# Loading the constants first and running the first chunk's step size, input product and first scan tile by tile

## The chip, the cores and the metric

The kernel runs on one core of a Trainium2 chip. What counts is the device time of one execution in microseconds; the time given for a kernel is the median of its runs.

## What is computed

x holds 2 sequences of 1024 tokens of 256 features. Rows of small norm are masked, a Mamba block (in-projection, causal convolution, selective scan with 16 states, gate, out-projection) runs on them, then an attention block with a modulated query and a gated feed-forward. The part that the change touches is the front of the Mamba block:

```python
rows_to_keep = clip((sigmoid(cond @ score_w + score_b) * 1024).astype(int32), 1, None)
thresholds = sort(norm(x))[::-1][rows_to_keep - 1]          # rows below are zeroed
xn = rmsnorm(x_masked, rms_w)
xi, z = split(xn @ in_proj, 2)                              # 512 channels each
xi = silu(causal_conv4(xi) + conv_b)
dt, Bm, Cm = split(xi @ x_proj, [16, 32])
delta = softplus(dt @ dt_w + dt_b)
A = -exp(A_log)
def step(h, (d_t, x_t, B_t, C_t)):                          # over time, h: 512 x 16
    h = exp(d_t[..., None] * A) * h + (d_t * x_t)[..., None] * B_t[:, None, :]
    return h, einsum('bds,bs->bd', h, C_t)
y = (scan(step) + xi * D) * silu(z)
```

## The kernel before

Time is cut into four chunks of 512 steps (NCH = 4, two per sequence), the 512 channels into four tiles of 128 (CT = 4), and a chunk's scan into 16 states (NS). One scan step n is one state of one chunk: for each of the four tiles ScalarE makes exp(delta * A) into one of two PSUM banks (L1259), GpSimd makes the input product dx * B into a ring of four slots (L1403), and VectorE runs the scan over 512 steps of time (L1727). TensorE turns the result (L834), ScalarE and VectorE multiply it by C's column (L1269, L1740 and L1747), and TensorE or VectorE sums over the states.

TensorE's other work is a list of jobs, each with a PSUM bank. Jobs alternate between two banks of `pp`, so a job waits until the one two places ahead of it has been read. The head's list is: T (transposes of x), F (the keep fraction), I (in-projection), V (convolution), X (x_proj), D 0 to D 3 (the step size before softplus), XT (B and C turned; its reading by ScalarE writes `CTs`, the rows of C). Z 0 and Z 1 (the gate's in-projection) stand beside step 0, Z 2 and Z 3 beside step 1. So XT waits for the reading of D 2, Z 0 for that of D 3, Z 1 for that of XT, and Z 2 for that of Z 0.

Every engine works its instructions off in the order in which they are written. In the head: SP loads x's first two chunks (L421), the vectors (L425), the constants with the identity matrix (L426), and then weights; TensorE first runs WARM_ZEROS products on zeros (L863), the transposes T, and the transposes of the squared norms (L857), which need four sums of squares from ScalarE and four from VectorE. VectorE counts with them which rows are kept (L1652). `first_softplus` on ScalarE takes D 0 and D 1 as a pair, then D 2 and D 3 (Abs at L1117 or L1120, Exp L1122, Ln L1124). VectorE's reading of D (L1538) ends softplus, and behind each pair one instruction multiplies by xi (L1543) for GpSimd. B's rows go over DRAM: SP writes them (L440) and loads them spread over the partitions, two states at a time (L448). Behind the four scans of step 0 VectorE reads Z 0 and Z 1 (L1530), then makes the mask row (L1703) and one count (L1652), and then scans step 1.

## Time and profile before

| | |
|---|---|
| median of 3 runs | 565.59 us (562.24 to 568.28) |
| the profiled execution's own time | 562.97 us |
| its span | 561.2 us |
| mean granted TensorE clock in the span | 0.929 |
| busy: TensorE matmuls, VectorE, GpSimd, ScalarE | 86%, 82%, 69%, 66% |
| chain that ended last: TensorE, VectorE, issue, ScalarE, GpSimd | 49%, 27%, 11%, 10%, 2% |

The share of busy time is that of an engine in the whole span. The chain is followed back from the last instruction to what released each step; an engine with a large share there sets the time. A granted clock of 1 is 2.4 GHz and one of 0.5 is 1.2 GHz.

### The profile page before, as it was taken

The page shows a single profiled execution, that of the slowest core. Times are in us where ns is not written, and L with a number is a line of the kernel's source. Part 1 is how long each engine was busy: PE and PEld are TensorE (multiplying, and loading weights), DVE is VectorE, ACT ScalarE, POOL GpSimd, SP SyncE. Part 2 cuts the span into 40 slices and gives each one's busy share as a digit, 9 for nine tenths or more (in the row PEclk, how much of TensorE's full clock was granted, in tenths as well). Part 3 has the DMA queues.
Part 4 walks back from the last instruction along what each step waited for, and adds up shares of the span by engine and source line. Part 5 has one row for each costly group of instructions (what it writes and reads, how often), then busy time and mean ns, then how long its engine had stood idle before and what let it go on. Part 6 is the DMA issues. An engine that isn't in the chain of part 4 may idle for free.

```text
span 561.2 us, 7944 instructions
## 1 busy us (share of the span) xinstructions
PE 481.0 (86%) x2777; PEld 348.8 (62%) x2777; DVE 461.2 (82%) x531; ACT 372.5 (66%) x650; POOL 387.2 (69%) x235
## 2 busy tenths in 40 slices
PE   8968999868768999987689999986897968899992
PEld 6423765455557665745576657656796856888651
DVE  4779989979999889799997897899998989851522
ACT  3676777769966767898757678897568668721210
POOL 5039978767996877879968778599789969510001
PEclk9987999979989999899899999598998869799997
DMA  8330111111111001111010111111111590029004
GB/s 289 115 116 38 39 38 39 40 40 37 39 37 39 38 39 39 40 39 39 39 39 37 39 37 41 38 38 38 39 39 39 201 369 1 2 87 353 2 1 155
DMA packets 17919, 38.88 MB, mean 69 GB/s; under 512 B 1665, under 2 KB 10497, under 8 KB 17874
## 3 DMA queue, kind: packets, MB, share of 16 engines
q1 hardware_dynamic: 17874, 38.32, 19.8%
q8 instruction: 24, 0.39, 0.3%
q14 instruction: 21, 0.17, 0.1%
HBM read 36.08 MB, written 2.23 MB: 68 GB/s over the span
## 4 chain that ended last, share of the span: by engine, by line
PE 49%; DVE 27%; issue 11%; ACT 10%; POOL 2%; DVEq 0%; ACTq 0%; POOLq 0%
DVE scanmem L1727 16%; PE hT L834 11%; PE pp L563 6%; PE pp L539 6%; PE yacc L597 5%; DVE yTd L1747 5%; PE pp L626 4%; ACT dA L1259 2%; PE dA L799 2%; PE pp L575 2%; PE pp L589 2%; ACT hc L1269 1%; PE pp L770 1%; PE pp L649 1%; DVE yTd L1652 1%
## 5 line engine op out<-in xcount | busy, mean ns | idle before, releaser
L1403 POOL TENSOR_TENSOR scanmem<-par,scanmem 128x1024 f32<-128x1024 f32 x128 | 300.9, 2370 | 79.7 <-PE hT L834 60.3
L834 PE MATMUL hT<-con,scanmem 128*128 128x128 f32 x1024 | 167.4, 298 | 54.0 <-DVE yTd L1747 32.0
L1259 ACT ACTIVATE dA<-par,Aneg 128x512 f32<-128x512 f32 x256 | 171.7, 690 | 56.0 <-DVE scanmem L1727 54.5
L834 PEld LDWEIGHTS hT<-con,scanmem 128*128 128x128 f32 x1024 | 126.7, 152 | 108.2 <-issue 34.3
L1727 DVE TENSOR_TENSOR_SCAN scanmem<-dA,carry,scanmem 128x512 f32<-128x512 f32 x128 | 156.7, 1266 | 11.9 <-ACT dA L1259 11.7
L1727 DVE TENSOR_TENSOR_SCAN scanmem<-dA,scanmem 128x512 f32<-128x512 f32 x128 | 148.9, 1204 | 8.5 <-ACT dA L1259 7.8
L1269 ACT ACTIVATE hc<-hT,CTs 128x512 f32<-128x512 f32 x128 | 87.1, 680 | 43.5 <-PE hT L834 43.3
L597 PE MATMUL yacc<-con,hc 128*128 128x128 f32 x512 | 86.6, 297 | 0.3 <-ACT hc L1269 0.3
L597 PEld LDWEIGHTS yacc<-con,hc 128*128 128x128 f32 x512 | 69.4, 157 | 0.6 <-ACT hc L1269 0.6
L1747 DVE SCALAR_TENSOR_TENSOR yTd<-hT,CTs,yTd 128x512 f32<-128x512 f32 x85 | 62.0, 729 | 8.4 <-PE hT L834 7.5
L539 PE MATMUL pp<-xnT,wi 128*128 128x512 f32 x120 | 59.0, 620 | 3.4 <-ACT xnT L1038 2.1
L563 PE MATMUL pp<-xr,diag 128*128 128x512 f32 x112 | 50.2, 592 | 0.0
L1463 POOL TENSOR_TENSOR par<-xt,hc 128x1024 f32<-128x1024 f32 x1 | 2.4, 2350 | 53.0 <-ACT hc L1319 53.0
L539 PEld LDWEIGHTS pp<-xnT,wi 128*128 128x128 f32 x120 | 21.6, 198 | 22.2 <-issue 17.4
L563 PEld LDWEIGHTS pp<-xr,diag 128*128 128x128 f32 x112 | 20.3, 189 | 21.1 <-issue 20.9
L626 PE MATMUL pp<-wo,par 128*128 128x256 f32 x128 | 29.0, 381 | 0.5 <-DVE par L1507 0.5
L1415 POOL TENSOR_TENSOR yTd<-yTd,sm 128x512 f32<-128x512 f32 x21 | 26.9, 1280 | 0.0
L626 PEld LDWEIGHTS pp<-wo,par 128*128 128x128 f32 x128 | 23.8, 190 | 3.9 <-DVE par L1507 0.7
L1415 POOL TENSOR_TENSOR yTd<-yTd,xnT 128x512 f32<-128x512 f32 x14 | 17.8, 1274 | 8.1 <-ACT xnT L1278 8.1
L589 PE MATMUL pp<-dbc,wdt 17*128 17x512 f32 x28 | 17.3, 706 | 0.4 <-DVE xt L1553 0.3
L1538 DVE SCALAR_TENSOR_TENSOR par<-pp,par 128x512 f32<-128x512 f32 x14 | 9.6, 688 | 9.3 <-ACT par L1130 6.4
L799 PE MATMUL dA<-con 128*128 128x128 f32 x110 | 17.1, 289 | 0.0
(195 smaller groups left out, 510.8 us busy)
## 6 DMA issues: line engine op xcount, KB each, us to landing
scanmem<-brow SPq DMA_DIRECT2D x32, 512.0 KB, 3.6
par<-in SPq DMA_DIRECT2D x1, 4096.0 KB, 17.3
scanmem<-in SPq DMA_DIRECT2D x1, 4096.0 KB, 15.0
xt<-in SPq DMA_DIRECT2D x4, 512.0 KB, 6.7
wi<-in SPq DMA_DIRECT2D x2, 1024.0 KB, 6.7
out<-par SPq DMA_DIRECT2D x4, 512.0 KB, 4.1
aw<-in SPq DMA_DIRECT2D x5, 256.0 KB, 6.7
xr<-in SPq DMA_DIRECT2D x1, 1024.0 KB, 8.9
```

The costliest lines, as they stand in the source:

```text
L539: last = mm(o, win[:, k, col:col + P], xnT[:, k, :], start=k == 0, stop=k == KD - 1)
L563: last = mm(o, dg[:, m, k, :], xr3[:, m, k:k + T], start=k == 0, stop=k == KC - 1)
L589: return mm(o, wdt[:, m * P:(m + 1) * P], dbc[0:DR + 1, :], start=True, stop=True)
L597: return mm(o[:, m * P:(m + 1) * P], src, ident, start=False, stop=last, is_transpose=True, skip_group_check=True)
L626: last = mm(o[:, i * DM:(i + 1) * DM], dx(e)[:, m, t0:t0 + P], wo[:, m, :], start=m == 0, stop=m == CT - 1)
L834: last = nc.tensor.transpose(hT[:, i % 2, m * P:(m + 1) * P], hb[:, n % RING, m, i * P:(i + 1) * P], ident)
L1259: A(dA[:, m % 2, :], delta(c)[:, m, :], ACT.Exp, scale=Aneg[:, m * NS + s:m * NS + s + 1]).then_inc(da_ready, 1)
L1269: A(hc[:, e % 2, :], hT[:, 0, :], ACT.Copy, scale=CTs[:, c % 2, i, s:s + 1]).then_inc(mul_done, 1)
L1403: nc.gpsimd.tensor_tensor(hb[:, n % RING, ms, :], dx(c)[:, ms, :], Bb[:, row:row + 1, :].to_broadcast([P, 2, T]), ALU.mult).then_inc(bx_re ...
L1415: nc.gpsimd.tensor_tensor(dst, dst, for_pool(n), ALU.add).then_inc(pool_sum_done, 1)
L1727: V.tensor_tensor_scan(hb[:, n % RING, m, :], dA[:, m % 2, :], hb[:, n % RING, m, :], start, ALU.mult, ALU.add).then_inc(scan_done, 1)
L1747: V.scalar_tensor_tensor(dst, src, cs, dst, ALU.mult, ALU.add).then_inc(mac_done, 1)
```

## The change

Five things are changed.

- SP loads the constants first of all, ahead of x, on a semaphore of their own (`s_con`). TensorE's transposes wait for that one alone; ScalarE waits for the vectors ahead of its reading of T, GpSimd for the vectors and then for the constants.
- WARM_ZEROS is 5 instead of 8.
- `first_softplus` takes one tile at a time; VectorE multiplies each tile by xi by itself, and GpSimd makes the first input product of step 0 in four instructions of one tile (`first_input_step`) instead of two of two tiles.
- The exponentials and scans of step 0 are moved in between those tiles.
- ScalarE reads XT (C's rows) behind the four exponentials of step 0 instead of ahead of them.

```diff
-WARM_ZEROS = 8
+WARM_ZEROS = 5
...
+            sp.dma_start(con[:, :], consts).then_inc(s_con, 16)
             load_x(0)
             load_x(1)
             sp.dma_start(vec[:, :], vecs).then_inc(s_vec, 16)
-            sp.dma_start(con[:, :], consts).then_inc(s_vec, 16)
...
-            def first_softplus(pair):
+            def first_softplus(m):
 
-                d = delta(0)[:, 2 * pair:2 * pair + 2, :]
-                if pair == 0:
-                    for m in range(2):
-                        wait_full(act, ("D", 0, m))
-                        own.mark(A(delta(0)[:, m, :], bank(("D", 0, m)), ACT.Abs))
-                else:
-                    wait_full(act, ("D", 0, 3))
-                    own.mark(A(d, hT[:, :, :], ACT.Abs))
+                d = delta(0)[:, m, :]
+                wait_full(act, ("D", 0, m))
+                own.mark(A(d, bank(("D", 0, m)), ACT.Abs))
...
+            first_softplus(0)
+            first_softplus(1)
+            exp_step(0, 0)
+            first_softplus(2)
+            exp_step(0, 1)
+            first_softplus(3)
+            exp_step(0, 2)
+            exp_step(0, 3)
+            read(("XT", 0, 0))
...
+            def first_input_step():
+
+                pool.wait_ge(bb_in[0], 16)
+                for m in range(CT):
+                    pool.wait_ge(dx_ready, m + 1)
+                    nc.gpsimd.tensor_tensor(hb[:, 0, m, :], dx(0)[:, m, :], Bb[:, 0, :], ALU.mult).then_inc(bx_ready, 1)
...
-                if n == 0 and m % 2:
-                    wait_read(dve, ("D", 0, m - 1))
+                if n == 0:
                     wait_read(dve, job)
-                    ms = slice(m - 1, m + 1)
-                    V.tensor_tensor(dx(0)[:, ms, :], delta(0)[:, ms, :], xi(0)[:, ms, :], ALU.mult).then_inc(dx_ready, 2)
+                    V.tensor_tensor(dx(0)[:, m, :], delta(0)[:, m, :], xi(0)[:, m, :], ALU.mult).then_inc(dx_ready, 1)
...
+            read(("D", 0, 0))
+            read(("D", 0, 1))
+            scan_step(0, 0)
+            read(("D", 0, 2))
+            scan_step(0, 1)
+            read(("D", 0, 3))
+            scan_step(0, 2)
+            scan_step(0, 3)
```

ScalarE around the first softplus, before, from the Abs of D 0 and D 1 to the reading of Z 0 and Z 1 (L1117 to L1124 softplus, L1089 C's rows, L1259 the exponentials of step 0, L1102 the tanh of Z with its table load):

```order
L1117 ACTIVATE par<-pp 128x512 x2
L1122 ACTIVATE par<-par 128x1024
L1124 ACTIVATE par<-par 128x1024
L1120 ACTIVATE par<-hT 128x1024
L1122 ACTIVATE par<-par 128x1024
L1124 ACTIVATE par<-par 128x1024
L1089 ACTIVATE CTs<-pp 128x64
L1259 ACTIVATE dA<-par,Aneg 128x512 x4
L1102 ACT_TABLE_LOAD
L1102 ACTIVATE par<-pp 128x512 x2
```

The same place in the changed kernel, behind the softplus of D 0 and D 1 (L1120 to L1124 softplus, L1255 the exponentials, L1094 C's rows, L1107 Z):

```order
L1255 ACTIVATE dA<-par,Aneg 128x512
L1120 ACTIVATE par<-hT 128x512
L1122 ACTIVATE par<-par 128x512
L1124 ACTIVATE par<-par 128x512
L1255 ACTIVATE dA<-par,Aneg 128x512
L1120 ACTIVATE par<-hT 128x512
L1122 ACTIVATE par<-par 128x512
L1124 ACTIVATE par<-par 128x512
L1255 ACTIVATE dA<-par,Aneg 128x512 x2
L1094 ACTIVATE CTs<-pp 128x64
L1107 ACT_TABLE_LOAD
L1107 ACTIVATE par<-pp 128x512 x2
```

Two exponentials now stand ahead of the end of softplus, and C's rows are read behind all four.

VectorE before, from the reading of D 0 to the mask row (L1538 the reading of D, L1543 the product with xi, L1727 the scans of step 0, L1530 the reading of Z, L1703 the mask row, L1652 a count):

```order
L1538 SCALAR_TENSOR_TENSOR par<-pp,par 128x512 x2
L1543 TENSOR_TENSOR par<-par 128x1024
L1538 SCALAR_TENSOR_TENSOR par<-hT,par 128x512 x2
L1543 TENSOR_TENSOR par<-par 128x1024
L1727 SCALAR_TENSOR_TENSOR scanmem<-dA,scanmem 128x512 x4
L1530 SCALAR_TENSOR_TENSOR par<-par,pp 128x512 x2
L1703 TENSOR_SCALAR negm<-x1T 128x1024
L1652 TENSOR_SCALAR yTd,cnt<-x1T,ss 128x1024
```

VectorE in the changed kernel, from the reading of D 1 on (L1556, L1559, L1742, L1548 and L1716 are the same things in the same order):

```order
L1556 SCALAR_TENSOR_TENSOR par<-pp,par 128x512
L1559 TENSOR_TENSOR par<-par 128x512
L1742 SCALAR_TENSOR_TENSOR scanmem<-dA,scanmem 128x512
L1556 SCALAR_TENSOR_TENSOR par<-hT,par 128x512
L1559 TENSOR_TENSOR par<-par 128x512
L1742 SCALAR_TENSOR_TENSOR scanmem<-dA,scanmem 128x512
L1556 SCALAR_TENSOR_TENSOR par<-hT,par 128x512
L1559 TENSOR_TENSOR par<-par 128x512
L1742 SCALAR_TENSOR_TENSOR scanmem<-dA,scanmem 128x512 x2
L1548 SCALAR_TENSOR_TENSOR par<-par,pp 128x512 x2
L1716 TENSOR_SCALAR negm<-x1T 128x1024
```

The reading of D 3 now stands behind the first two scans.

## Rows read from the trace of the kernel before

**Rows 1.** The page: its first line, the span.
```profile
span 561.2 us, 7944 instructions
```

**Rows 2.** The chain that ended last, in order of time: start us, us, what.
```profile
9.71 1.30 DVE yTd L1652 x2
...
16.13 0.65 PE hT L876 x4
...
55.52 0.73 DVE yTd L1740
```

**Rows 3.** Timeline of ScalarE: start us, us, instruction; the last sum of squares.
```profile
7.28 0.18 ACT L1203 ACTIVATION_READ_ACCUMULATOR scanmem<-xt 128x1 f32 x1
```

**Rows 4.** Timeline of TensorE: products on zeros; first weight loads of L857.
```profile
1.51 6.41 PE L863 MATMUL hT<-a_sb 128*128 128x256 f32 x16 [1.51 <-POOL z_sb L1369]
...
8.52 0.90 PEld L857 LDWEIGHTS yacc<-con,ss 128*128 128x128 f32 x8
```

**Rows 5.** Timeline of SP's queue: issue of x, of the constants, of B's rows.
```profile
0.74 1.01 SPq L421 DMA_DIRECT2D xt<-in  x2
...
2.33 0.43 SPq L426 DMA_DIRECT2D con<-in  x1
...
34.92 1.28 SPq L448 DMA_DIRECT2D scanmem<-brow  x3
```

**Rows 6.** Timeline of ScalarE, from the first Abs to the reading of Z.
```profile
34.58 0.60 ACT L1117 ACTIVATE par<-pp 128x512 f32<-128x512 f32 x1 [0.31 <-PE pp L589]
...
40.24 1.06 ACT L1124 ACTIVATE par<-par 128x1024 f32<-128x1024 f32 x1
...
47.60 1.28 ACT L1102 ACT_TABLE_LOAD   x1
48.89 1.08 ACT L1102 ACTIVATE par<-pp 128x512 f32<-128x512 f32 x2
```

**Rows 7.** Groups by line and shape, ScalarE: busy us, mean ns | idle before.
```profile
L1130 ACT ACTIVATE par<-par 128x512 f32<-128x512 f32 x12 | 7.6, 630 | 0.4
```

**Rows 8.** Timeline of VectorE, from the first product with xi to the mask row.
```profile
39.74 1.23 DVE L1543 TENSOR_TENSOR par<-par 128x1024 f32<-128x1024 f32 x1
41.40 1.29 DVE L1538 SCALAR_TENSOR_TENSOR par<-hT,par 128x512 f32<-128x512 f32 x2 [0.44 <-ACT par L1124]
42.83 1.73 DVE L1543 TENSOR_TENSOR par<-par 128x1024 f32<-128x1024 f32 x1
...
47.08 2.34 DVE L1727 TENSOR_TENSOR_SCAN scanmem<-dA,scanmem 128x512 f32<-128x512 f32 x2 [0.28 <-POOL scanmem L1403]
49.59 1.28 DVE L1530 SCALAR_TENSOR_TENSOR par<-par,pp 128x512 f32<-128x512 f32 x2 [0.18 <-ACT par L1102]
50.80 1.35 DVE L1703 TENSOR_SCALAR negm<-x1T 128x1024 f32<-128x1024 uint8 x1
```

**Rows 9.** DMA issues by line: KB each, median us from issue to landing.
```profile
scanmem<-brow SPq DMA_DIRECT2D x32, 512.0 KB, 3.6
```

**Rows 10.** Groups by line and shape, GpSimd: a product of one tile.
```profile
L1440 POOL TENSOR_TENSOR par<-par 128x512 f32<-128x512 f32 x12 | 15.1, 1284 | 0.0
```

**Rows 11.** Timeline of TensorE: Z 0 and Z 1, then Z 2 and Z 3.
```profile
42.75 6.27 PE L539 MATMUL pp<-xnT,wi 128*128 128x512 f32 x8
50.34 3.70 PE L539 MATMUL pp<-xnT,wi 128*128 128x512 f32 x8 [1.32 <-DVE par L1530]
```

**Rows 12.** Stretches: each engine's busy us (instructions), then granted clock, DMA share, GB/s.
```profile
47.50:48.00 0.50, 0.50 (x2) 0.02 (x2) 0.50 (x1) 0.48 (x2) 0.50 (x1) 0.55 0.00 0
```

**Rows 13.** Timeline of TensorE from 116 us, and the granted clock of two stretches there.
```profile
116.76 1.11 PE L834 MATMUL hT<-con,scanmem 128*128 128x128 f32 x4 [3.75 <-DVE yTd L1747]
117.67 1.06 PE L597 MATMUL yacc<-con,hc 128*128 128x128 f32 x4
...
116.00:117.00 1.00, 0.24 (x1) 0.24 (x2) 1.00 (x3) 0.90 (x2) 0.02 (x1) 0.61 0.00 0
...
119.00:120.00 1.00, 1.00 (x7) 0.86 (x5) 0.78 (x1) 1.00 (x3) 0.28 (x1) 0.69 0.04 16
```

More of the change, by code:

```diff
@@ L168, in vector_sums, with products_of_inputs @@
     return 2 * n + (i + 1) // 2 - pool_sums(n if i == 3 else n - 1)
+def products_of_inputs(n, pair):
+    return CT + 2 * (n - 1) + pair + 1
 def to_read(h):
@@ L329, in build @@
         brow = nc.dram_tensor("brow", [NCH, NS, T], F32, kind="Internal").ap()
-        s_vec, s_w, s_aw, s_mrow = sem("vec_in"), sem("w_in"), sem("aw_in"), sem("mrow_in")
+        s_vec, s_con, s_w, s_aw, s_mrow = sem("vec_in"), sem("con_in"), sem("w_in"), sem("aw_in"), sem("mrow_in")
         s_x = [sem(f"x_in{i}") for i in range(NCH)]
@@ L444, in _ @@
                     if piece >= BSLOTS:
-                        sp.wait_ge(bx_ready, 2 * BROWS * (piece - BSLOTS + 1))
+                        sp.wait_ge(bx_ready, products_of_inputs(BROWS * (piece - BSLOTS + 1) - 1, 1))
                     slot = piece % BSLOTS
@@ L495, in job_F @@
             def job_F(job, o):
-                pe.wait_ge(s_vec, 32)
+                pe.wait_ge(s_vec, 16)
                 for b in range(B):
@@ L526, in job_T @@
                         pe.wait_ge(s_x[0], 16)
-                        pe.wait_ge(s_vec, 32)
+                        pe.wait_ge(s_con, 16)
                     for i in range(NT):
@@ L1210, in _ @@
             A(xr3[:, :, 0:KC - 1], zero[:, :, :], ACT.Copy).then_inc(halo_ready, 1)
+            act.wait_ge(s_vec, 16)
             for k in range(KD):
@@ L1225, in _ @@
             A(fr[:, 1, :], fr[:, 0, :], ACT.Exp, scale=-1.0).then_inc(fe_ready, 1)
-            act.wait_ge(s_vec, 32)
             A(Aneg[:, :], v("A_log"), ACT.Exp).then_inc(aexp_ready, 1)
@@ L1243, in _ @@
                 A(magrow[:, i * 512:(i + 1) * 512], hT[:, i, :], ACT.Copy).then_inc(mag_act, 1)
-            for pair in range(CT // 2):
-                first_softplus(pair)
-            read(("XT", 0, 0))
             def exp_step(n, m):
@@ L1288, in _ @@
                     n = c * NS + s
-                    exp_step(n, 0)
-                    exp_step(n, 1)
+                    if n:
+                        exp_step(n, 0)
+                        exp_step(n, 1)
                     if n >= 2:
@@ L1296, in _ @@
                         read(job)
-                    exp_step(n, 2)
-                    exp_step(n, 3)
                     if n:
+                        exp_step(n, 2)
+                        exp_step(n, 3)
                         mul_step(n - 1, 0)
@@ L1369, in _ @@
             nc.gpsimd.memset(z_sb[:, :, :], 0.0).then_inc(pads_zero, 1)
-            pool.wait_ge(s_vec, 32)
+            pool.wait_ge(s_vec, 16)
             nc.gpsimd.tensor_scalar(half_b[:, :], v("conv_b"), 0.5, 1.0, ALU.mult, ALU.mult).then_inc(half_ready, 1)
             nc.gpsimd.tensor_scalar(half_w[:, :], v("conv_w"), 0.5, 1.0, ALU.mult, ALU.mult).then_inc(half_ready, 1)
+            pool.wait_ge(s_con, 16)
             for m in range(CT):
@@ L1446, in _ @@
                         row_scaling(c + 1)
-                    input_step(n, 0)
+                    if n:
+                        input_step(n, 0)
                     if n >= RING:
                         add_step(n - RING)
-                    input_step(n, 1)
+                    if n:
+                        input_step(n, 1)
+                    else:
+                        first_input_step()
                     for m in POOL_ENDS:
@@ L1536, in ev_D @@
                 else:
-                    dve.wait_ge(head_sp_ready, m // 2 + 1)
+                    dve.wait_ge(head_sp_ready, m + 1)
                 V.scalar_tensor_tensor(delta(n)[:, m, :], o, 0.0, delta(n)[:, m, :], ALU.max, ALU.add).then_inc(freed(job), 1)
-                if n == 0 and m % 2:
-                    wait_read(dve, ("D", 0, m - 1))
+                if n == 0:
                     wait_read(dve, job)
-                    ms = slice(m - 1, m + 1)
-                    V.tensor_tensor(dx(0)[:, ms, :], delta(0)[:, ms, :], xi(0)[:, ms, :], ALU.mult).then_inc(dx_ready, 2)
+                    V.tensor_tensor(dx(0)[:, m, :], delta(0)[:, m, :], xi(0)[:, m, :], ALU.mult).then_inc(dx_ready, 1)
                 return None
@@ L1695, in _ @@
             V.tensor_scalar(Aneg[:, :], Aneg[:, :], -1.0, None, ALU.mult).then_inc(A_ready, 1)
-            for m in range(CT):
-                read(("D", 0, m))
             def batch1_rows(s):
@@ L1717, in scan_step @@
                 dve.wait_ge(da_ready, i + 1)
-                if m % 2 == 0:
-                    dve.wait_ge(bx_ready, 2 * n + m // 2 + 1)
+                if n == 0:
+                    dve.wait_ge(bx_ready, m + 1)
+                elif m % 2 == 0:
+                    dve.wait_ge(bx_ready, products_of_inputs(n, m // 2))
                 if c % HALVES:
@@ L1751, in _ @@
                     n = c * NS + s
-                    scan_step(n, 0)
-                    scan_step(n, 1)
+                    if n:
+                        scan_step(n, 0)
+                        scan_step(n, 1)
                     if n:
@@ L1757, in _ @@
                         read(job)
-                    scan_step(n, 2)
-                    scan_step(n, 3)
                     if n:
+                        scan_step(n, 2)
+                        scan_step(n, 3)
                         mac_step(n - 1, 3)
```

## The prediction

> **What bounds the kernel now.** I read the page first, then the chain of waits from its start to 60 us, then the timelines of the single engines around each piece of that chain that the change touches, and last the granted clock. The page gives a span of 561.2 us [rows 1]. The change touches only the first 50 us, so the question is how much earlier (or later) the steady loop starts.
>
> The chain in the head starts with the warm-up products on zeros and the eight transposes of x. Behind them come the transposes of the squared norms, L857, and the counting on VectorE, L1652, from 9.71 [rows 2]. What could have been first? ScalarE's last sum of squares reads out at 7.28 plus 0.18, so 7.46 [rows 3]; the squares alone would have let L857 begin there. It began at 8.52 (its first weight load [rows 4]), because the eight products on zeros and the transposes were still in TensorE's queue. From the counting on, everything up to the step-size products follows in one chain.
>
> The end of the head is a second place. VectorE runs without a pause from the Z readings L1530 at 49.59, over the mask row L1703 at 50.80, to the first sum L1740 at 55.52, which the chain names and behind which TensorE goes on with its transposes [rows 2, 8]. The scans of state 0 are ahead of all this. So the loop is released by the time at which VectorE has read Z 0 and Z 1, and not by the scans alone.
>
> **The change part by part: the loads and the zeros.** Three of eight products on zeros go. Each is two instructions, and the sixteen took 6.41 us [rows 4], 0.40 each for 256 columns, nearly what 512 columns take at full clock further on (0.46, eight in 3.70 [rows 11]); so the clock was low for most of them, though the view of the granted clock has no entry that early. Three are worth 2.4 us of TensorE's queue. x is then what is waited for: the transposes end before the squares do. L857 can start at 7.46 plus the delay that the constants now give x. On SP the two loads of x took 1.01 us to issue and the one of the constants 0.43 [rows 5]; a load put ahead delays the others by about 0.45. Gain: 8.52 - 7.46 - 0.45 = 0.6 us. Bounds: 1.06 if x is not delayed at all, 0.16 if it is delayed by twice that. The waits that are moved (ScalarE on the vectors before it reads the transposes; GpSimd on vectors, then constants) come due at about the time x does; 14 us of later work cover GpSimd's diagonals. The early I products need not be quicker: their results wait for the counting.
>
> **The first softplus, tile by tile.** Before, a pair takes an Abs of 0.60 for each tile and an Exp and a Ln of 1.06 for both [rows 6]. Now each tile takes Abs 0.60, Exp 0.63 and Ln 0.63 (the 512-wide form of later chunks, of which the Ln is shown; the Exp has the same mean [rows 7]), 1.9 us with the handovers. In the old run's times:
> - tile 0: Abs at 34.58, Ln done at 36.50; VectorE reads it (0.69) and multiplies (0.62, half of 1.23) until 37.9 [rows 8].
> - tile 1: Ln done 38.3. First exponential for the scan (0.69) until 38.95. Rows of B: the load of them was issued at 34.92 [rows 5] and lands 3.6 us later [rows 9], 38.5, so GpSimd can start its first tile there, 1.28 us each [rows 10], and ends at about 39.7.
> - VectorE: tile 1 until 39.9 (its product slows when GpSimd runs: the second one took 1.73 against 1.23 [rows 8]), first scan 40.0 to 41.2, tile 2 until 42.7, second scan to 43.95.
> - tile 3: Ln done at 43.24 (behind tile 2 and the second exponential), but VectorE reads it only behind the second scan: 43.95 to 44.64. Then its product to 45.3, third scan to 46.6, fourth (behind GpSimd's tile 3, 46.8) to 48.05.
>
> What VectorE and GpSimd take from each other is a disputed price. The row shows 0.5 us more for 1024 columns while GpSimd worked beside it [rows 8], so 0.25 for a tile, and I count it once; two such products stand ahead of the reading of tile 3. Bounds: nothing, or a whole GpSimd instruction of 1.28 for each of the two [rows 10], which makes tile 3 2.3 us later than my walk. The Trainium skill, GPSIMD Engine Reference, 8. Key points, says that GpSimd shares its SBUF interfaces with VectorE and contends with its instructions that have two SBUF inputs, and gives no size; if the two took turns entirely, the sum would be at the upper bound, by the row it is near the lower. The rule speaks against a change that puts such products of both engines side by side, and the trace agrees that there is a price.
>
> The four scans ended at 49.42 before (the last two started at 47.08 and took 2.34 [rows 8]). They are 1.4 us earlier, 2.0 with the gain above. That is what the change buys on VectorE.
>
> **What it costs.** Z 0 uses the PSUM bank that tile 3 of D leaves. Before, VectorE left tile 3 at 42.69 [rows 8] and Z 0 and Z 1 started at 42.75. Now tile 3 is left at 44.64, behind two scans: 1.95 us later. C's rows are read behind the fourth exponential, at 44.7, just in time for Z 1. TensorE had done little for five microseconds, its clock was at half and came back only at 47.9, so the two jobs took 6.27 us, where Z 2 and Z 3, the same eight products, took 3.70 at full clock [rows 11, 12]. With the same 6.27 they end at 50.97. ScalarE's reading (0.60) and VectorE's (0.67, and handovers) follow: 52.3, where before VectorE was through at 50.87, because ScalarE, with its table load from 47.60 to 48.88 behind the last exponential, was nearly as late as Z [rows 6]. The scans' gain is idle time of VectorE now: it waits for Z 1. Sum: +1.45 - 0.6 = **+0.85 us**. Bounds of the disputed term: with 3.70 for the two jobs Z 1 is ready at 48.4, and the sum is -1.7; the first products still run at half clock after such an idle time in this trace, and I take the row of these very jobs.
>
> 562.97 + 0.85 = 563.8 on the scale of the profiled execution. It lies 2.6 us under the median of the three runs, 565.59 (562.24 to 568.28), so the forecast is 566.4. A difference within 1% (5.7 us) is about what a measurement of this kernel can't tell from none, and the largest gain that I can construct in the head is 1.06 + 1.4 = 2.5 us.
>
> **The rivals.**
> 1. The forecast: Z 1 is late, the scans' gain is lost, no measurable difference. 566.4. Chance 0.42.
> 2. The clock comes back early in Z 0, or stays up: VectorE has Z 1 read at about 49.1 instead of 50.87: -1.7 us, 561.2 for the profile, 563.9. For it: when the clock rises has no fixed relation to these jobs. Against: in the trace the jobs had run for 5.2 us when it rose [rows 12]. Chance 0.25.
> 3. Slower, the clock in the head: fewer zeros leave TensorE quiet between the transposes and L857, and the clock is low from there. L857 takes twice 0.89, and the first I pair as long as the Z pair, 6.27 instead of 3.70 [rows 11]. It decides if that pair ends later than 15.5, when TensorE can turn the rows' scale (16.13 before [rows 2], less the gain): from about 10.5 it would end at 16.8, 1.3 late. With 0.9 for L857 the head loses 2.2 against my sum: +3, or 568.6. Against: at 116.76 TensorE began, at half clock behind a long pause, a stretch of turning only (L834, L597), and at 119.6 the clock rose to full [rows 13]; the same kind of work, the transposes, now stands behind the five products on zeros. Chance 0.12.
> 4. Slower, VectorE against GpSimd: both products ahead of the reading of tile 3 wait for a whole GpSimd instruction, 2.3 us; Z 0 and Z 1 follow by as much: +3.1, 568.7. It decides once the products of VectorE take more than about 1.2 instead of 0.62. Against: the row's 0.5 for 1024 columns. Chance 0.06.
> 5. The head does not change: the constants ahead delay x by a whole microsecond, so that the zeros gone gain nothing, and Z is late: +1.45, 567.0. Chance 0.07.
> 6. A shift of the loop moves TensorE's stretches at half clock. The table's mean clock of 0.929 is 14% of the span, 80 us, at half; a tenth or so of that more or fewer, with some of TensorE's work in it on the chain, is a few microseconds; the three runs of before already spread over 6 us. This alone can carry the time past 1%, to either side. Chance 0.08.
>
> **How the numbers follow.** Cases 1, 2 and 5 lie between 563.9 and 567, cases 3 and 4 near 568.6; the spread of single runs is 3 us to each side. The range for 8 in 10 is 561.5 to 570. Over 1% faster (below 559.9) only case 6 with luck, or case 2 together with a fast median: 0.05. Over 1% slower (above 571.2): case 6, or case 3 or 4 with a slow median: 0.06. Within 1%: 0.89.
>
> **What would show it.** L857's first weight load near 7.9; counting on VectorE from about 9.1 (step one). The first scan about 4 us earlier than 44.47, and four scans with gaps between them (step two). Z 0 starting at about 44 behind the reading of tile 3 of D, and VectorE idle before its reading of Z 1, with TensorE named as the releaser (step three). The mask row at about 51.6 against 50.80: if it comes at 49 or earlier, the step on the clock was wrong; if L1652 starts later than 9.7, the step on the loads or zeros was.

## The result, and the profile after

Twenty runs of each kernel on one chip: 562.44 us before (558.79 to 568.57), 566.48 us after (563.0 to 571.83), ratio 1.0091 with an interval of 1.0066 to 1.0116. The ratio and the table of the experiments leave out those runs of a kernel that lie over 1.5% above its fastest (here 5 of before and 2 of after), and so the ratio gives 5.1 us (3.7 to 6.5) where the medians of all twenty lie 4.0 apart. The change thus stays under the 1% that I had set as the limit of a difference, but it is slower: the whole interval lies above 1. The forecast of 566.4 was met by luck: the three runs of before that I started from had a median 3 us above that of twenty. I had forecast +0.85 us, and the change costs five to six times that.

The profiled execution of after is its slowest of twenty (571.83), so its end is not compared with before's. I compare places in the first chunk, above all the end of the fourth scan of a step: from step 4 to step 9 its distance to the same place in before's profile stays the same within 0.01 us in every profile, so it tells how far the head has moved the steps behind it. For after it is +4.05 us.

The chain that ended last, of the changed kernel (start us, us, what):

```profile
8.07 1.09 PE yacc L862 x8
...
11.50 5.37 PE dA L544 x8
16.86 0.44 PE hT L881 x4
...
44.04 1.22 DVE scanmem L1742
45.25 0.59 DVE par L1556
45.89 9.20 PE pp L544 x16
...
56.57 2.25 DVE scanmem L1742 x2
58.82 0.65 DVE yTd L1755
```

The Z jobs (L544, four of them without a pause) stand in the chain, behind VectorE's second scan and its reading of D 3 (L1556). In the chain before, the two first scans of step 0, an exponential of ScalarE, its table load and its reading of Z 0 stood in that place, and only Z 2 and Z 3 behind them. The other end of the piece, the first sum (L1755), starts at 58.74 in the timeline where it was 55.52 [rows 2].

The timeline of VectorE there (start us, us, instruction, idle time before it and what ended it):

```profile
41.59 1.22 DVE L1742 TENSOR_TENSOR_SCAN scanmem<-dA,scanmem 128x512 f32<-128x512 f32 x1 [1.23 <-POOL scanmem L1417]
...
44.04 1.22 DVE L1742 TENSOR_TENSOR_SCAN scanmem<-dA,scanmem 128x512 f32<-128x512 f32 x1
45.17 0.67 DVE L1556 SCALAR_TENSOR_TENSOR par<-hT,par 128x512 f32<-128x512 f32 x1
45.87 0.69 DVE L1559 TENSOR_TENSOR par<-par 128x512 f32<-128x512 f32 x1
46.48 1.22 DVE L1742 TENSOR_TENSOR_SCAN scanmem<-dA,scanmem 128x512 f32<-128x512 f32 x1
48.00 1.22 DVE L1742 TENSOR_TENSOR_SCAN scanmem<-dA,scanmem 128x512 f32<-128x512 f32 x1 [0.31 <-POOL scanmem L1417]
50.40 0.69 DVE L1548 SCALAR_TENSOR_TENSOR par<-par,pp 128x512 f32<-128x512 f32 x1 [1.18 <-ACT par L1107]
52.34 0.69 DVE L1548 SCALAR_TENSOR_TENSOR par<-par,pp 128x512 f32<-128x512 f32 x1 [1.25 <-ACT par L1107]
52.95 2.42 DVE L1716 TENSOR_SCALAR negm<-x1T 128x1024 f32<-128x1024 uint8 x1
55.29 1.27 DVE L1668 TENSOR_SCALAR_CACHE_REDUCE yTd<-x1T,ss 128x1024 f32<-128x1024 f32 x1
...
56.49 2.33 DVE L1742 TENSOR_TENSOR_SCAN scanmem<-dA,scanmem 128x512 f32<-128x512 f32 x2
58.74 0.72 DVE L1755 TENSOR_SCALAR yTd<-hT,CTs 128x512 f32<-128x512 f32 x1
```

These rows answer to [rows 8]. The scans end at 49.22, hardly before the old 49.42. Then VectorE idles 1.18 and 1.25 us ahead of its two readings of Z (before 0.18), and the mask row (L1716) starts at 52.95 against 50.80 and takes 2.42 us against 1.35.

ScalarE, which VectorE waits for, itself waits for TensorE (against [rows 6]):

```profile
46.72 1.28 ACT L1107 ACT_TABLE_LOAD   x1
49.70 0.60 ACT L1107 ACTIVATE par<-pp 128x512 f32<-128x512 f32 x1 [1.70 <-PE pp L544]
51.65 0.60 ACT L1107 ACTIVATE par<-pp 128x512 f32<-128x512 f32 x1 [1.34 <-PE pp L544]
```

TensorE (against [rows 4, 11]): the weight loads of L862, the first I pair, the Z jobs, and the two halves of step 0's transposes:

```profile
8.07 0.85 PEld L862 LDWEIGHTS yacc<-con,ss 128*128 128x128 f32 x8 [1.49 <-ACT scanmem L1203]
...
11.50 5.37 PE L544 MATMUL dA<-xnT,wi 128*128 128x512 f32 x8 [1.00 <-issue]
...
45.89 9.18 PE L544 MATMUL pp<-xnT,wi 128*128 128x512 f32 x16 [1.78 <-DVE par L1556]
54.91 1.04 PE L839 MATMUL hT<-con,scanmem 128*128 128x128 f32 x8
59.51 1.80 PE L839 MATMUL hT<-con,scanmem 128*128 128x128 f32 x8 [3.57 <-DVE yTd L1755]
```

Stretches (each engine's busy us and instructions, then the granted clock, DMA share, GB/s):

```profile
15.00:16.00 1.00, 1.00 (x3) 0.48 (x2) 0.46 (x3) 0.00 (x0) 0.00 (x0) 0.57 1.10 348
...
48.00:50.00 2.00, 2.00 (x3) 0.77 (x3) 1.22 (x1) 0.30 (x2) 2.00 (x1) 0.50 0.00 0
50.00:52.00 2.00, 2.00 (x6) 0.88 (x5) 0.69 (x1) 0.66 (x2) 2.00 (x2) 1.00 0.00 0
...
62.50:63.00 0.50, 0.50 (x4) 0.50 (x4) 0.50 (x2) 0.08 (x2) 0.50 (x1) 0.50 0.00 0
```

The Z jobs run at half clock until about 50. The transposes behind VectorE's first sum start after a pause of 3.57 us (before: 1.38), and for some 3 us from 60 on the clock is at half, which it was not before: the eight transposes take 1.80 against 1.35.

SP's loads of B's rows (against [rows 5]):

```profile
35.44 1.28 SPq L453 DMA_DIRECT2D scanmem<-brow  x3
```

GpSimd's products (L1417 a tile of step 0, L1410 a pair of later steps), each piece as it stands in the timeline of a window:

```profile
39.78 1.70 POOL L1417 TENSOR_TENSOR scanmem<-par,scanmem 128x512 f32<-128x512 f32 x1 [6.14 <-DMA scanmem<-brow]
...
50.16 4.66 POOL L1410 TENSOR_TENSOR scanmem<-par,scanmem 128x1024 f32<-128x1024 f32 x2
...
52.47 5.11 POOL L1410 TENSOR_TENSOR scanmem<-par,scanmem 128x1024 f32<-128x1024 f32 x2
```

The two pair products of the first of these rows start at 50.16 and end at 54.82 (the second starts at 52.47); the last row holds that second one and the next, and the next alone thus takes 5.11 - 2.31 = 2.80 us, where the others take 2.35. That next one is the one that runs when the mask row ends, at 52.95 + 2.42 = 55.37. Why this matters is the second half of this document.

### The profile page after: what moved, and what is told of

The parts are those of the page before. It is cut to its first block, busy times and chain, and to the rows that moved or that the text cites. A ratio compares the mean times of both kernels' runs of the same rounds, so it can differ in the third digit from the quotient of the medians.

```text
span 570.0 us, 7942 instructions
## 1 busy us (share of the span) xinstructions
PE 491.1 (86%) x2771; PEld 356.2 (62%) x2771; DVE 463.0 (81%) x533; ACT 373.7 (66%) x655; POOL 387.9 (68%) x237
## 4 chain that ended last, share of the span: by engine, by line
PE 54%; DVE 22%; issue 10%; ACT 8%; POOL 4%; DMA 1%; DVEq 0%; SPq 0%; ACTq 0%; POOLq 0%
PE hT L839 13%; DVE scanmem L1742 13%; PE pp L544 7%; PE pp L568 6%; PE yacc L602 6%; DVE yTd L1762 4%; PE pp L631 4%; PE pp L594 3%; POOL scanmem L1410 2%; ACT dA L1255 2%; PE dA L804 2%; PE pp L580 2%; PE pp L775 1%; PE pp L654 1%; PE yacc L598 1%
## 5 line engine op out<-in xcount | busy, mean ns | idle before, releaser
L1410 POOL TENSOR_TENSOR scanmem<-par,scanmem 128x1024 f32<-128x1024 f32 x126 | 296.1, 2368 | 78.7 <-PE hT L839 69.0
L839 PE MATMUL hT<-con,scanmem 128*128 128x128 f32 x1024 | 170.0, 302 | 52.4 <-DVE yTd L1762 29.6
L1255 ACT ACTIVATE dA<-par,Aneg 128x512 f32<-128x512 f32 x256 | 171.8, 690 | 57.0 <-DVE scanmem L1742 53.9
L839 PEld LDWEIGHTS hT<-con,scanmem 128*128 128x128 f32 x1024 | 130.1, 155 | 107.4 <-issue 39.2
L1742 DVE TENSOR_TENSOR_SCAN scanmem<-dA,carry,scanmem 128x512 f32<-128x512 f32 x128 | 156.9, 1269 | 11.6 <-ACT dA L1255 11.3
L1742 DVE TENSOR_TENSOR_SCAN scanmem<-dA,scanmem 128x512 f32<-128x512 f32 x128 | 149.4, 1209 | 10.1 <-ACT dA L1255 8.2
L602 PE MATMUL yacc<-con,hc 128*128 128x128 f32 x512 | 88.5, 302 | 0.3 <-ACT hc L1265 0.3
L602 PEld LDWEIGHTS yacc<-con,hc 128*128 128x128 f32 x512 | 70.6, 159 | 0.6 <-ACT hc L1265 0.6
L544 PE MATMUL pp<-xnT,wi 128*128 128x512 f32 x120 | 58.9, 620 | 3.9 <-ACT xnT L1043 2.1
L544 PEld LDWEIGHTS pp<-xnT,wi 128*128 128x128 f32 x120 | 22.0, 203 | 22.3 <-issue 16.8
L594 PE MATMUL pp<-dbc,wdt 17*128 17x512 f32 x28 | 21.0, 845 | 0.4 <-DVE xt L1569 0.3
L1556 DVE SCALAR_TENSOR_TENSOR par<-pp,par 128x512 f32<-128x512 f32 x14 | 9.7, 691 | 9.5 <-ACT par L1130 7.9
```

The costliest lines, as they stand in the source:

```text
L544: last = mm(o, win[:, k, col:col + P], xnT[:, k, :], start=k == 0, stop=k == KD - 1)
L594: return mm(o, wdt[:, m * P:(m + 1) * P], dbc[0:DR + 1, :], start=True, stop=True)
L602: return mm(o[:, m * P:(m + 1) * P], src, ident, start=False, stop=last, is_transpose=True, skip_group_check=True)
L839: last = nc.tensor.transpose(hT[:, i % 2, m * P:(m + 1) * P], hb[:, n % RING, m, i * P:(i + 1) * P], ident)
L1255: A(dA[:, m % 2, :], delta(c)[:, m, :], ACT.Exp, scale=Aneg[:, m * NS + s:m * NS + s + 1]).then_inc(da_ready, 1)
L1410: nc.gpsimd.tensor_tensor(hb[:, n % RING, ms, :], dx(c)[:, ms, :], Bb[:, row:row + 1, :].to_broadcast([P, 2, T]), ALU.mult).then_inc(bx_re ...
```

## The experiments

"B's load" is where SP issues the first load of B's rows (before 34.92), "scans" where the two first scans of step 1 start (before 53.27), "step 9" the distance to before at the end of its fourth scan. Below the first row the ratio is of 12 runs of the kernel (6 of tiles_only) against 29 or 35 of before beside them.

| kernel | ratio to before, interval | B's load | mask row: start, us | scans | step 9 |
|---|---|---|---|---|---|
| after | 1.0091 [1.0066, 1.0116] | 35.44 | 52.95, 2.42 | 56.49 | +4.05 |
| after_zeros8 | 1.0062 [1.0021, 1.0103] | 35.04 | 51.59, 2.85 | 55.55 | +2.80 |
| head_only | 1.0007 [0.9963, 1.0051] | 34.84 | 50.72, 1.34 | 53.18 | -0.08 |
| tiles_only | 1.0101 [1.0038, 1.0164] | 34.30 | 52.44, 1.79 | 55.35 | +2.09 |
| d3_first | 1.0020 [0.9978, 1.0062] | 35.61 | 52.12, 2.55 | 55.78 | +3.35 |
| mask_first | 0.9997 [0.9963, 1.0030] | 34.87 | 48.57, 1.61 | 52.50 | +0.72 |
| early_rows | 0.9987 [0.9953, 1.0021] | 34.37 | 34.95, 0.69 | 52.21 | -0.69 |
| before_early_rows | 0.9968 [0.9935, 1.0001] | 34.26 | 34.83, 0.69 | 50.13 | -1.63 |
| after_warm | 1.0085 [1.0056, 1.0114] | 34.78 | 51.98, 2.74 | 55.84 | +3.29 |
| before_swap | 1.0071 [1.0032, 1.0111] | 34.78 | 51.86, 2.47 | 54.25 | +1.61 |
| after_swap | 1.0052 [1.0012, 1.0093] | 34.69 | 52.78, 1.30 | 54.00 | +0.73 |
| combined | 0.9994 [0.9953, 1.0035] | 34.85 | 35.42, 0.68 | 50.54 | -1.39 |

The head by itself does not come out the same from execution to execution. Of the edits below only the zeros and the order of the loads act ahead of B's load, and yet it is issued at 34.26 to 35.04 in the six profiles with eight zeros. So up to 0.8 us of a distance at step 9 need not be the edit's. Less the difference at B's load it is 3.53 for after, 2.68 for after_zeros8, 2.71 for tiles_only, 2.66 for d3_first, 1.75 for before_swap and 0.96 for after_swap.

**The two halves of the change.** after_zeros8 puts the zeros back:

```diff
-WARM_ZEROS = 5
+WARM_ZEROS = 8
```

> The changed kernel with WARM_ZEROS back at 8, all else as changed. Theory Z (the slowdown comes from the readings: tile 3 of D is read behind two scans, so Z 0, Z 1 and the mask row come late): little changes, still 0.6 to 1.0% over the kernel before; the mask row starts 2 us later than before's 50.80 less what the head gains. Theory H (the slowdown comes from too few products on zeros: the clock falls at about 12 us and the first I pair takes 5.4 us instead of 3.7): the I pair takes 3.7 in the profile and the time comes back to within 0.4% of before.

head_only is the kernel before with the constants loaded first and five zeros:

```diff
-WARM_ZEROS = 8
+WARM_ZEROS = 5
...
+            sp.dma_start(con[:, :], consts).then_inc(s_con, 16)
             load_x(0)
             load_x(1)
             sp.dma_start(vec[:, :], vecs).then_inc(s_vec, 16)
-            sp.dma_start(con[:, :], consts).then_inc(s_vec, 16)
...
```

> The kernel before with the head part alone: constants first and WARM_ZEROS 5, softplus in pairs as before. Theory Z: no slower than before, 0 to 0.2% faster, because the counting starts 0.5 us earlier. Theory H: slower by 0.3 to 0.9%, with the first I pair at 5.4 us and the turning of the rows' scale at 16.7 instead of 16.1.

tiles_only is the rest of the change, with the loads and the eight zeros as before:

```diff
-            for pair in range(CT // 2):
-                first_softplus(pair)
...
+            first_softplus(0)
+            first_softplus(1)
+            exp_step(0, 0)
+            first_softplus(2)
...
```

> The kernel before with the tile-by-tile part alone (softplus, first product, exponentials and scans of step 0 interleaved, C's rows behind them), loads and 8 zeros as before. Theory Z: the whole slowdown is here, 0.6 to 1.0% over before, mask row at 52.5 to 53.5 against 50.80. Theory H: within 0.4% of before, although the mask row is late by 1 to 2 us.

The tiles are the main cost: alone they give 1.0101, and their interval lies above 1; the head alone gives 1.0007, and its interval holds 1. tiles_only has six runs, its interval is wide (2.1 to 9.2 us) and overlaps that of head_only a little, so that it is as slow as after is not shown; but its mask row is 1.64 us late where that of head_only is not late. What the head gains at the counting (9.48 against 9.71 in head_only) is 0.08 at the first Abs of softplus.

The clock in the first I pair, rival 3, is a matter of the execution: the pair took 5.37 instead of 3.67 us in the profiles of after and d3_first, 3.67 in those of head_only, mask_first, early_rows, after_warm and after_swap, all seven with five zeros; and 3.67 in the six profiles with eight. With the fall B's load is issued at 35.44 and 35.61, without it at 34.37 to 34.87 with five zeros: about 0.8 us. With eight zeros the changed kernel is 1.25 us earlier at step 9, but only 0.40 of it is there at B's load, and 0.47 more come from the load, which took 3.80 us to land instead of 4.27. The intervals of the two ratios overlap, so that the time does not decide between the two cases of the expectation.

**The order on VectorE.** d3_first reads D 3 ahead of the second scan, so that Z 0 gets its bank earlier:

```diff
-            scan_step(0, 1)
             read(("D", 0, 3))
+            scan_step(0, 1)
             scan_step(0, 2)
```

> The changed kernel with one line moved: VectorE reads tile 3 of D ahead of the second scan instead of behind it, so that Z 0's bank is free 1.2 us earlier. Theory Z: Z 0 starts at about 44.6 instead of 45.9, the mask row 1 to 1.3 us earlier than in the changed kernel, and 1 to 3 us of the 4 to 5 us come back. Theory H: the time stays at the changed kernel's, 0.9% over before.

TensorE in this kernel:

```profile
44.69 9.66 PE L544 MATMUL pp<-xnT,wi 128*128 128x512 f32 x16 [0.76 <-DVE par L1556]
```

Z 0 starts 1.20 us earlier than in after although this profile has the slow I pair too, the scans of step 1 0.71 earlier, and the time falls by some 4 us (1.1 over before against 5.1). The intervals of the two ratios just do not overlap. So the late bank is a part of the loss, and reading D 3 behind the second scan was the costly place. The time gained is more than the profile accounts for (0.70 at step 9).

mask_first makes the mask row and the count behind the scans of step 0, ahead of the readings of Z:

```diff
+                    if n == 0:
+                        batch1_rows(0)
                     for job in to_read(2 * n + 1):
                         read(job)
-                    if c == 0:
+                    if c == 0 and n:
                         batch1_rows(s)
```

> The changed kernel with the mask row and its count moved ahead of VectorE's reading of Z 0 and Z 1, into the time in which it waits for them. Theory V (the loss is VectorE's chain behind the Z readings: Z late, then a mask row that is held until GpSimd's running instruction ends): the first scan of state 1 starts at 53 to 54 instead of 56.5, and 2 to 3.5 us come back, to 0.2 to 0.5% over before. Rival T (the loss is TensorE's late Z 2 and Z 3 and its clock): reading Z later makes it worse, 1% or more over before.

early_rows puts the same two instructions ahead of the reading of D 0, where GpSimd does nothing:

```diff
+            batch1_rows(0)
             read(("D", 0, 0))
             read(("D", 0, 1))
             scan_step(0, 0)
...
-                    if c == 0:
+                    if c == 0 and n:
                         batch1_rows(s)
```

> The changed kernel with the mask row and its count ahead of the reading of tile 0 of D, while GpSimd has nothing to do. Theory V, with the shared access: the mask row takes 0.6 to 0.8 us instead of 2.42, the first scan of state 1 follows the reading of Z 1 at about 53, and the time is 0 to 0.3% over before. If the mask row's length came from its data or its form and not from GpSimd, it takes 1.3 to 2.5 here too and pushes the reading of tile 0 back by 1 to 2 us.

before_early_rows does the same to the kernel before:

```diff
-            for m in range(CT):
-                read(("D", 0, m))
...
+            batch1_rows(0)
+            for m in range(CT):
+                read(("D", 0, m))
...
-                    if c == 0:
+                    if c == 0 and n:
                         batch1_rows(s)
```

> The kernel before with the mask row and its count in VectorE's pause ahead of the reading of D 0 (2.7 us). Theory V: the mask row takes 0.6 to 0.8 instead of 1.35, scans of state 1 start at about 50.9 instead of 53.3, but the first sum then waits for TensorE's Z 2 and Z 3 (done at 54): 0.5 to 1 us faster, 0.1 to 0.2%. If VectorE alone set the pace there, 2.5 us or 0.45% faster.

VectorE in early_rows: the mask row and the count, a product with xi, the second reading of Z, the scans:

```profile
34.95 0.69 DVE L1716 TENSOR_SCALAR negm<-x1T 128x1024 f32<-128x1024 uint8 x1
35.55 1.27 DVE L1668 TENSOR_SCALAR_CACHE_REDUCE yTd<-x1T,ss 128x1024 f32<-128x1024 f32 x1
...
38.79 1.64 DVE L1559 TENSOR_TENSOR par<-par 128x512 f32<-128x512 f32 x1
...
51.60 0.69 DVE L1548 SCALAR_TENSOR_TENSOR par<-par,pp 128x512 f32<-128x512 f32 x1 [1.76 <-ACT par L1107]
52.21 2.33 DVE L1742 TENSOR_TENSOR_SCAN scanmem<-dA,scanmem 128x512 f32<-128x512 f32 x2
```

In mask_first the two instructions fill the time in which VectorE idled ahead of Z (its readings then follow without a wait); in early_rows that idle time stays, and they are gone from behind it. Either way after's 5.1 us over before vanish (0.9997 and 0.9987). The kernel before has less to gain: VectorE is 3.1 us earlier at the scans of step 1, but has to wait 1.38 us for TensorE's transposes ahead of the first sum, and 1.63 is left at step 9, of which 0.66 was there at B's load. The mask row takes 0.69 us where GpSimd rests.

**The clock.** after_warm fills TensorE's pause between D 3 and XT with ten products on the identity:

```diff
                 run(("D", 0, m))
+            pe.wait_ge(ranked, 2)
+            keep_warm(10, yacc[:, 0, 0:P])
             run(("XT", 0, 0))
```

> The changed kernel with ten products of the identity (into a bank of yacc that is free then) between D 3 and XT, so that TensorE is busy through most of its pause. If half clock in Z 0 and Z 1 is what makes Z 1 late: the pair takes 3.7 to 4.5 instead of 5.5 to 6.3, the mask row starts 1 to 2 us earlier and 1 to 3 us come back. If the late bank alone counts: the same time as the changed kernel, 0.9% over before.

Its stretches from 40 to 48 us (the clock ahead of the last two numbers):

```profile
40.00:42.00 2.00, 2.00 (x11) 2.00 (x11) 1.06 (x1) 1.97 (x4) 2.00 (x2) 0.50 0.30 123
42.00:44.00 2.00, 1.13 (x9) 0.81 (x7) 1.97 (x4) 1.56 (x3) 0.52 (x2) 0.93 0.00 0
44.00:46.00 2.00, 0.76 (x2) 0.48 (x3) 1.97 (x4) 0.78 (x2) 0.82 (x2) 0.93 0.00 0
46.00:48.00 2.00, 2.00 (x4) 0.81 (x3) 1.69 (x2) 1.33 (x2) 2.00 (x2) 0.50 0.00 0
```

The clock rose and, behind the pause between XT and Z 0 (1.99 us), fell again, so that Z ran at half all the same: 8.86 us for its sixteen products against 9.18. The ratio, 1.0085, did not move. So neither case of the expectation was tested, and what a full clock in Z would be worth stays open. That the pause that counts is the one ahead of Z 0, and so the late bank again, is argued from these rows and not shown.

**The exchange.** before_swap and after_swap exchange the mask row and the count behind it, in the kernel before and in the changed one:

```diff
-                    dve.wait_ge(s_mrow, 16)
-                    V.tensor_scalar(negm[:, :], mrow, -1.0, FLT_MAX, ALU.add, ALU.mult)
...
                     own.mark(count(GB + s, magrow, junk))
+                if s == 0:
+                    dve.wait_ge(s_mrow, 16)
+                    V.tensor_scalar(negm[:, :], mrow, -1.0, FLT_MAX, ALU.add, ALU.mult)
```

> The kernel before with two neighbours on VectorE exchanged in step 0: the count first, then the mask row; nothing else. If the mask row is held until GpSimd's running product ends: it starts at about 52.0 instead of 50.8, just behind the start of a product at 51.9, so it ends 0.25 behind that product's end at 54.3 and takes about 2.5 instead of 1.35; state 1 starts 1.1 us later, and the time rises by 0.2% or somewhat more. If its length has nothing to do with GpSimd: 1.35 again, and no change.

> The changed kernel with the same exchange. If GpSimd's products hold the mask row: it starts at 54.2 instead of 52.95 (in the changed kernel's profile), ends 0.25 behind the product that ends at 55.15, and takes about 1.2 instead of 2.42; state 1 starts 1.2 us earlier, and TensorE's pause ahead of its first transposes shrinks from 3.6 to 2.4: 1.2 to 3 us back, 0.4 to 0.7% over before. If not: no change, 0.9% over.

VectorE in before_swap, and GpSimd's products beside it:

```profile
50.66 1.27 DVE L1652 TENSOR_SCALAR_CACHE_REDUCE yTd<-x1T,ss 128x1024 f32<-128x1024 f32 x1
...
51.86 2.47 DVE L1709 TENSOR_SCALAR negm<-x1T 128x1024 f32<-128x1024 uint8 x1
54.25 2.32 DVE L1728 TENSOR_TENSOR_SCAN scanmem<-dA,scanmem 128x512 f32<-128x512 f32 x2
...
49.10 4.68 POOL L1403 TENSOR_TENSOR scanmem<-par,scanmem 128x1024 f32<-128x1024 f32 x2
```

and in after_swap:

```profile
51.58 1.27 DVE L1668 TENSOR_SCALAR_CACHE_REDUCE yTd<-x1T,ss 128x1024 f32<-128x1024 f32 x1
52.78 1.30 DVE L1722 TENSOR_SCALAR negm<-x1T 128x1024 f32<-128x1024 uint8 x1
54.00 2.33 DVE L1743 TENSOR_TENSOR_SCAN scanmem<-dA,scanmem 128x512 f32<-128x512 f32 x2
...
46.55 6.97 POOL L1410 TENSOR_TENSOR scanmem<-par,scanmem 128x1024 f32<-128x1024 f32 x3
```

The same two instructions, in the other order. From the start of the first of them to the scans of step 1 before took 2.47 us and takes 3.59 now; after took 3.54 and takes 2.42: 1.12 us, lost in the one and gained in the other. The length of the mask row went from 1.35 to 2.47 and from 2.42 to 1.30, as foretold (2.5 and 1.2). It depends on where it starts against GpSimd's products, and on nothing else that I changed. Behind it before is 0.98 us later at step 1, and 1.61 at step 9, because the clock now falls between 57 and 58 (pause ahead of the transposes 2.50). after_swap is 2.49 earlier than after at the scans, but 1.3 of that was there at the first scan of step 0 (40.29 against 41.59), ahead of the exchange; its clock does not fall (pause 2.45), and its ratio, 1.0052, is not clearly below that of after, as the intervals overlap.

**All together.** combined has eight zeros, D 3 read first and the early rows:

```diff
-WARM_ZEROS = 5
+WARM_ZEROS = 8
...
+            batch1_rows(0)
             read(("D", 0, 0))
...
-            scan_step(0, 1)
             read(("D", 0, 3))
+            scan_step(0, 1)
...
-                    if c == 0:
+                    if c == 0 and n:
                         batch1_rows(s)
```

> The changed kernel with the three repairs together: WARM_ZEROS 8, tile 3 of D read ahead of the second scan, the mask row and its count ahead of tile 0 of D. Theory V: Z 0 starts at 43.5 to 44, the scans of state 1 at 51 to 52 against 53.27 before, mask row 0.69; 0.2 to 0.6% faster than before. If the interleaving itself is worth nothing, it is level with the kernel before with early rows alone (0.3% faster) or behind it.

It is 1.39 us ahead of before at step 9 and no faster in time (0.9994); the 0.2 to 0.6% did not come, and that working tile by tile is worth anything here is not shown. None of the kernels beats before by more than its interval; the nearest is before_early_rows (0.9968, up to 1.0001), and it needs nothing of the change.

## What the mask row waits for

Two rows of the kernel before that my sum does not use, GpSimd's products beside [rows 8]:

```profile
41.11 2.35 POOL L1403 TENSOR_TENSOR scanmem<-par,scanmem 128x1024 f32<-128x1024 f32 x1 [7.99 <-DVE par L1543]
...
49.24 5.13 POOL L1403 TENSOR_TENSOR scanmem<-par,scanmem 128x1024 f32<-128x1024 f32 x2
```

The end of GpSimd's running product and that of the mask row, in all ten profiles in which it starts beside one:

| kernel | mask row starts | GpSimd's product ends | mask row ends | behind it |
|---|---|---|---|---|
| before | 50.80 | 51.60 | 52.15 | 0.55 |
| after | 52.95 | 54.82 | 55.37 | 0.55 |
| after_zeros8 | 51.59 | 53.89 | 54.44 | 0.55 |
| head_only | 50.72 | 51.50 | 52.06 | 0.56 |
| tiles_only | 52.44 | 53.67 | 54.23 | 0.56 |
| d3_first | 52.12 | 54.11 | 54.66 | 0.55 |
| mask_first | 48.57 | 49.63 | 50.18 | 0.55 |
| after_warm | 51.98 | 54.17 | 54.72 | 0.55 |
| before_swap | 51.86 | 53.78 | 54.33 | 0.55 |
| after_swap | 52.78 | 53.53 | 54.08 | 0.55 |

So it does not run slower beside GpSimd; its end hangs on the end of GpSimd's instruction and comes 0.55 us behind it, however long it has stood there. Alone it took 0.69, 0.14 more. GpSimd's next product is held in its turn (2.80 for 2.35). After starts 0.48 us behind the start of a product and ends 1.73 later than it would alone, before 0.66. The Trainium skill, SBUF — State Buffer, 🔬 SBUF: two separate sides, says just this: the port pair that VectorE and GpSimd share is "an **exclusive lock**, not a bandwidth split", held for a whole instruction by whoever starts first. Its section Who interferes with whom counts `tensor_scalar` among those that can take it (but not the form that also writes out its accumulator), and instructions with two SBUF inputs beside a GpSimd instruction that reads SBUF. The ten rows agree, 0.55 or 0.56 us each. The scans, which read one of their inputs from PSUM, take 1.22 each beside the same products (at 48.00 in after), as that section has it. And the count, as large as the mask row, from SBUF to SBUF and of that form with an accumulator, took 1.27 beside a product (at 55.29 in after) as where GpSimd rests (at 35.55 in early_rows): not every such instruction is held.

It holds for other rows. The product with xi of 1.73 us in [rows 8] started at 42.83; GpSimd's product ended at 41.11 + 2.35 = 43.46, and it ended 1.10 behind that, again 0.13 less than the 1.23 of the product that stood alone. In early_rows the product of 1.64 us at 38.79 ends at 40.43, 0.55 behind GpSimd's (38.62 + 1.26 = 39.88). In after VectorE's product of 39.66 came first and GpSimd's took 1.70 instead of 1.26. And a tiny instruction can be held as long as a large one, of after:

```profile
114.59 1.98 DVE L1672 TENSOR_SCALAR keep<-cnt,fr 128x8 f32<-128x8 f32 x1
...
114.20 2.35 POOL L1410 TENSOR_TENSOR scanmem<-par,scanmem 128x1024 f32<-128x1024 f32 x1 [2.94 <-PE hT L839]
```

It ends at 116.57, GpSimd's product at 116.55. This table was made after the last run: the exchange had both lengths foretold from the ends of GpSimd's products, and the exact 0.55 was read from the rows afterwards.

## Why the prediction was right or wrong

**The loads and the zeros: the wait right, the gain not there.** With five zeros L862 does wait for the squares, as foretold: in all seven profiles its first weight load comes 0.05 us behind ScalarE's last sum of squares, in after at 8.07 (7.9 foretold). In after the counting starts at 9.20, 0.5 earlier than before's 9.71 (0.6). But that start moves by itself from 9.05 to 9.83 in the six profiles with eight zeros and from 8.99 to 9.66 in the seven with five, with means of 9.48 and 9.36, and before's is one of the late ones. At B's load the means are 34.69 with eight and 34.71 with five at full clock. So the 0.6 of the sum is not there to be seen. The squares end 0.5 later on average with the constants ahead of x (8.19 against 7.72), as counted (0.45). But the sixteen products on zeros took 5.75 to 6.54 us in the six profiles, and before's 6.41, from which I worked out the rest, was one of the long ones.

In this execution rival 3 came too: its pair ended at 16.87, foretold 16.8, for about 0.8 us at B's load instead of the 1.3. With 0.12 I gave it too little; it stood in two of seven profiles with five zeros. The argument against it, that turning alone had raised the clock at 119.6 [rows 13], says when a clock rises, not that it stays when a pause follows. It doesn't decide the result: tiles_only has eight zeros and the pair at 3.67, and the loss is there.

**The tiles: right in kind, 2.2 us late.** The first scan came at 41.59. My walk had it at 39.4 (40.0 less the gain). 1.1 of the difference is the head (0.5 late instead of 0.6 early: B's load is issued at 35.44, not at 34.3), 0.7 the load (39.78, so 4.3 us behind its issue; 3.6 was the median of all the loads, but this very load had taken 4.2 in the trace of before, where two more of its kind are issued right behind it as well), 0.4 the product that was held for VectorE. From the first scan to the end of the reading of D 3 it went as foretold (4.25 us, foretold 4.64).

**Z behind the reading of D 3: right.** Z 0 starts at 45.89, foretold about 44.1, later by 1.8: the first scan's 2.2 less the 0.4 of the shorter walk. Z 0 and Z 1 at half clock took 5.76 us until ScalarE could read Z 1 (6.27 taken), and the scans' gain turned into VectorE's idle time ahead of Z, TensorE the releaser. d3_first bears it out. Rival 2 did not come: the clock came back at about 50, and in none of the thirteen profiles was the pair near 3.70 (5.2 to 6.3). The mask row comes at 52.95, foretold about 51.6. The excess of 1.3 is the 1.8 by which Z 0 was late, less 0.5 for the shorter Z pair.

**The step that failed: the sum ended at the start of the mask row.** I wrote "+0.85" for how late VectorE is through with Z and took what stands behind as a block of fixed length. It isn't. Of the 3.2 us that are missing at step 9, 1.3 are the terms above, the head's first, and 1.9 stand behind that place:

| | us at step 9 |
|---|---|
| mask row starts later: 52.95 - 50.80 (foretold 0.85) | +2.15 |
| mask row is longer: 2.42 - 1.35 | +1.07 |
| TensorE's clock falls ahead of step 3 | +0.8 |
| sum | +4.0 |

Measured +4.05 at step 9. The second line follows from the rule above. [rows 8] with GpSimd's row would have shown its kind, an end set by GpSimd, though not its size: that hangs on where in a product of 2.35 us the mask row starts, and I had its start wrong by 1.3. Rival 4 had the mechanism, VectorE waiting for a whole GpSimd instruction, but put it on the products with xi, where it did not strike in after (0.69 us for each of the four). There GpSimd's product of a tile waits for VectorE's, so that the two mostly take turns by themselves; but the one of 1.64 in early_rows shows that it can. And I had dismissed it with "the row's 0.5 for 1024 columns", a remaining wait read as a rate. For the same reason the prediction's choice between "a share" and "turns" went the wrong way, although what it costs there is small.

The third line comes from the longer pause of TensorE, 3.57 against 1.38: its next transposes wait for VectorE's first sum, and that is late by 3.2. Pauses of 3.58 to 3.99 in three other kernels and one of 2.50 in before_swap had the same end; one of 2.45 in after_swap and one of 2.94 in tiles_only had not. That the fall made these 0.8 us is read from the rows, and no run took it away by itself. A prediction can't place this to a microsecond, but whoever makes such a pause longer should price the slower clock behind it.

**Open: the rest of the time.** Measured differences are mostly larger than the distance at step 9: +5.1 against 4.05 for after, +4.0 (1.8 to 6.2) against 1.61 for before_swap, +2.9 (0.7 to 5.2) against 0.73 for after_swap. From step 10 on the distances change again, in both directions, and but for 0.37 us that come at step 21 and go at step 22 only where the two profiles differ in their stretches at half clock: before_swap stands at +8.2 at step 36 and at +1.7 at the end of the last scan, and tiles_only at -2.0. after_swap, whose profile has thirteen stretches at half clock as before's has, at the same places and as long, keeps its distance: 0.73 at step 9 and 0.59 at the end of the last scan. That is rival 6, which I gave 0.08. That such stretches make the surplus is argued from single profiles and not shown; no run fixed them.

## What to carry to other kernels

What an engine gains ahead of a hand-over of a bank can be lost when the reading that frees the bank is put behind the gained work: place the reading first. Some VectorE instructions from SBUF to SBUF (here the mask row, the product with xi and one on 128x8 elements, but not the count) cost what is left of the GpSimd product beside them, so put such a one where GpSimd rests (here 0.69 us instead of up to 2.85), and read a length that varies for one shape against the ends of GpSimd's instructions. Carry a sum on until the distance stays constant, here step 4, and not only to the last instruction that was moved; take the time before from more than three runs where a difference of a few microseconds is asked for; and read a gain of half a microsecond in the head from several profiles, for this head moved by 0.8 without a change.

## What the runs showed of the hardware

- One and the same instruction of VectorE on 128x1024 elements, the mask row, took 0.68 or 0.69 us in the three kernels in which GpSimd rested beside it, and 1.30 to 2.85 in the ten in which a product ran, always ending 0.55 or 0.56 behind that product. One on 128x8 elements took 1.98. The count on 128x1024 took 1.27 either way.
- With the same loads and zeros, the clock in the first I pair fell in two profiles (5.37 us) and stayed in five (3.67): the program alone does not settle it.
- In after_warm the clock had risen from 42 on (0.93 in two stretches) and was at half from 46 on, with a pause of 1.99 us between XT and Z 0 ahead of the fall.
